# Triangle attention scores: head by head on small tiles of the array, instead of one product with an expanded q

## The reference

```
B, N, _, E = x_in.shape            # 2, 64, 64, 256
H = 8;  d_k = E // H               # 8 heads of 32 channels
q = (x_in @ Wq).reshape(B, N, N, H, d_k)
k = (x_in @ Wk).reshape(B, N, N, H, d_k)
v1 = (x_in @ Wv1).reshape(B, N, N, H, d_k)
v2 = (x_in @ Wv2).reshape(B, N, N, H, d_k)
scores = jnp.einsum('bilhd,bljhd->biljh', q, k) / np.sqrt(d_k)
att = jax.nn.softmax(scores, axis=2)
out = jnp.einsum('biljh,bilhd,bljhd->bijhd', att, v1, v2)
attn_out = out.reshape(B, N, N, E) @ Wo
h = _layer_norm(x_in + attn_out, ln_agg_g, ln_agg_b)
mlp = jax.nn.relu(h @ W1 + b1) @ W2 + b2
return _layer_norm(mlp + h, ln_out_g, ln_out_b)
```

## Time and profile before

| what | value |
|---|---|
| median of three executions | 5114.2 us (5111.48 to 5121.49) |
| the profiled execution | 5109.28 us, its span 5107.6 us |
| PE busy | 4717.0 us, 92% of the span |
| DVE busy | 3492.3 us, 68% |
| ACT busy | 2556.8 us, 50% |
| POOL busy | 2226.1 us, 44% |
| mean granted TensorE clock | 0.965 of full speed |
| score matmuls, line 348 | 1024 records, 385 ns each, 124.6 us of PE busy time |

### The profile page before, as it was taken

How to read it: one execution, slowest core, us unless ns; L and a number is a source line. 1 busy time by engine, 2 the same in 40 slices (tenths; PEclk the granted TensorE clock), 3 DMA queues, 4 the chain that set the end, 5 groups by cost and what they waited for, 6 DMA issues and landing times. The chain is left out here.

```text
span 5107.6 us, 210897 instructions
## 1 busy us (share of the span) xinstructions
PE 4717.0 (92%) x87600; PEld 4048.9 (79%) x87600; DVE 3492.3 (68%) x5697; ACT 2556.8 (50%) x6424; POOL 2226.1 (44%) x1165
## 2 busy tenths in 40 slices
PE   7899989999958999999789999997899989899966
PEld 6788867888845999999569999996788877788866
DVE  3688854888834666666546666663688864788866
ACT  4676646676612333333223333333666746676633
POOL 0599950999933000000320000000499970899930
PEclk9999999999978999999899999998999999999988
DMA  2000011000012000000210000002100012000012
GB/s 80 24 24 24 24 40 52 22 24 24 23 55 69 16 15 15 15 15 12 66 48 16 15 15 15 13 12 70 33 24 24 24 32 60 21 24 24 24 55 86
DMA packets 183401, 162.51 MB, mean 32 GB/s; under 512 B 23472, under 2 KB 178608, under 8 KB 183216
## 3 DMA queue, kind: packets, MB, share of 16 engines
q1 hardware_dynamic: 183216, 159.94, 10.3%
HBM read 109.53 MB, written 50.33 MB: 31 GB/s over the span
## 5 line engine op out<-in xcount | busy, mean ns | idle before, releaser
L812 POOL TENSOR_TENSOR tri_work<-tri_v,tri_work 128x1024 f32<-128x1024 f32 x768 | 1802.5, 2378 | 154.9 <-PE tri_psum L567 154.5
L736 DVE TENSOR_TENSOR tri_work<-tri_v,tri_psum 128x1024 f32<-128x1024 f32 x1280 | 1506.8, 1218 | 215.0 <-PE tri_psum L567 195.0
L567 PE MATMUL tri_psum<-tri_work 128*32 128x64 f32 x65536 | 1104.7, 221 | 39.4 <-issue 17.0
L567 PEld LDWEIGHTS tri_psum<-tri_work 128*32 128x32 f32 x65536 | 964.0, 110 | 197.2 <-issue 105.1
L1238 ACT ACTIVATE global_work<-global_psum 128x512 f32<-128x512 f32 x512 | 306.6, 599 | 1011.7 <-PE global_psum L1199 1011.7
L1313 POOL TENSOR_TENSOR global_work<-global_work,global_bp 128x256 f32<-128x256 f32 x64 | 46.4, 745 | 1576.1 <-DVE global_work L1270 1568.5
L1276 DVE TENSOR_REDUCE global_work<-global_work 128x1 f32<-128x512 f32 x512 | 349.2, 682 | 472.3 <-ACT global_work L1238 472.3
L1219 PE MATMUL global_psum<-global_v_high,global_pT_high 128*128 128x256 f32 x2048 | 610.2, 298 | 4.1 <-DVE global_pT_low L1294 4.1
L1219 PE MATMUL global_psum<-global_v_high,global_pT_low 128*128 128x256 f32 x2048 | 577.1, 282 | 0.0
L1219 PE MATMUL global_psum<-global_v_low,global_pT_high 128*128 128x256 f32 x2048 | 576.7, 282 | 0.0
L1199 PE MATMUL global_psum<-global_k_high,global_q_high 128*128 128x512 f32 x1024 | 421.4, 412 | 24.3 <-DVE global_q_low L1256 21.5
(11 more groups left out here) (140 smaller groups left out, 7815.9 us busy)
## 6 DMA issues: line engine op xcount, KB each, us to landing
tri_work<-in_x SPq DMA_DIRECT2D x192, 128.0 KB, 2.1
tri_work<-x SPq DMA_DIRECT2D x192, 128.0 KB, 2.0
x<-tri_work SPq DMA_DIRECT2D x128, 128.0 KB, 1.7
tri_work<-in_x SPq DMA_DIRECT2D x128, 64.0 KB, 2.2
global_work<-x SPq DMA_DIRECT2D x16, 512.0 KB, 4.2
xn<-global_work SPq DMA_DIRECT2D x16, 512.0 KB, 3.0
qT<-global_work SPq DMA_DIRECT2D x32, 256.0 KB, 2.1
global_work<-qT SPq DMA_DIRECT2D x64, 128.0 KB, 2.2
```

What stands on the lines that cost most here:

```text
L567: mm = nc.tensor.matmul(psum[32 * g:32 * g + 32, OW, region * N:region * N + N], v1_diag[:, c * 32:c * 32 + 32], src[:, at_ * N:at_ * N + ...
L736: nc.vector.tensor_tensor(prod_d[k % 2].rearrange("p (d j) -> p d j", d=CU), v2[:, c:c + CU, :], psum[:, A[n.slot], (c // D) * N:(c // D + ...
L812: nc.gpsimd.tensor_tensor(prod_p[k % 2].rearrange("p (d j) -> p d j", d=CU), v2[:, c:c + CU, :], a_sb[n.slot][:, h * N:(h + 1) * N].unsque ...
```

## The change

q is copied as it is, in one copy on DVE into `qT`, which has the form of kT; the block-diagonal `q_diag`, its zeroing on POOL, the two copies on ACT and the two on DVE are gone, and with them their semaphores. The scores are made head by head: for each l, head r and half t one matmul over the 32 partitions of the head, 64 stationary and 64 moving columns, at the tile position (32 r, 64 t) of the array. That makes 32 matmuls in a group where there were 8. The head r picks the PSUM bank, 4 + r, of which the first 256 columns are used; bank 4 is also the bank of v2. So v2 of a group waits for the score copy of the group before it, and the scores of a group wait for the v2 copies of that group.

```diff
-        q_diag_all = part(2 * 2 * 4 * R * N)
-        q_diag = [q_diag_all[:, k * 8 * R * N:(k + 1) * 8 * R * N].rearrange("p (t l r i) -> p t l r i", t=2, l=4, r=R)
-                  for k in range(2)]
+        qT = [part(2 * 2 * P).rearrange("p (t n) -> p t n", t=2) for _ in range(2)]
...
-                s_psum = psum[:, 6:8, :].rearrange("p a n -> p (a n)")
+                s_psum = psum[:, 4:8, 0:E]
...
-                @block.gpsimd
-                def _(pool):
-
-                    nc.gpsimd.memset(q_diag_all, 0.0).then_inc(s["diag_zero"], 1)
...
-                            pe.wait_ge(s["v2_copy"], after(g - 1))
+                            pe.wait_ge(s["scores_copy"], after(g - 1))
...
-                            pe.wait_ge(s["q0_copy"], after(g))
-                            pe.wait_ge(s["q1_copy"], after(g))
-                            pe.wait_ge(s["scores_copy"], after(g - 1))
+                            pe.wait_ge(s["q_copy"], after(g))
+                            pe.wait_ge(s["v2_copy"], after(g))
                             for l in range(4):
-                                for t in range(2):
-                                    mm = nc.tensor.matmul(s_psum[N * t:N * t + N, l * R * N:(l + 1) * R * N],
-                                                          kT[g.slot][:, t, l * N:l * N + N],
-                                                          q_diag[g.slot][:, t, l].rearrange("p r i -> p (r i)"),
-                                                          start=True, stop=True)
+                                for r in range(R):
+                                    for t in range(2):
+                                        rows = slice(D * r, D * r + D)
+                                        mm = nc.tensor.matmul(s_psum[N * t:N * t + N, r, l * N:l * N + N],
+                                                              kT[g.slot][rows, t, l * N:l * N + N],
+                                                              qT[g.slot][rows, t, l * N:l * N + N],
+                                                              start=True, stop=True, tile_position=(D * r, N * t))
...
-                            if where is None:
-                                act.wait_ge(s["diag_zero"], b + 1 + CREDIT)
-                            for r in range(2):
-                                ins = q_copy(nc.scalar, nxt, r)
-                            ins.then_inc(s["q0_copy"], 1)
...
-                            nc.scalar.activation(scores[:, :, bass.ds((i * 2 + u) * 4, 4)],
-                                                 s_psum.rearrange("p (l n) -> p n l", l=4), ACT.Copy
+                            nc.scalar.activation(scores_i[:, :, :, bass.ds((i * 2 + u) * 4, 4)],
+                                                 s_psum.rearrange("p r (l i) -> p r i l", l=4), ACT.Copy
...
-                            dve.wait_ge(s["kT_copy"], after(nxt))
-                            if where is None:
-                                dve.wait_ge(s["diag_zero"], b + 1 + CREDIT)
-                            dve.wait_ge(s["q0_copy"], after(nxt))
-                            for r in range(2, R):
-                                rows = slice(D * r, D * r + D)
-                                ins = nc.vector.tensor_copy(q_diag[nxt.slot][rows, :, :, r, :],
-                                                            psum[rows, qk_bank[0], :].rearrange("p (t l i) -> p t l i", t=2, l=4))
-                            ins.then_inc(s["q1_copy"], 1)
+                            dve.wait_ge(s["scores_mm"], after(nxt - 2))
+                            nc.vector.tensor_copy(qT[nxt.slot], psum[:, qk_bank[0], :].rearrange("p (t n) -> p t n", t=2)
+                                                  ).then_inc(s["q_copy"], 1)
```

More of the change, by code:

```diff
@@ L234, in _ @@
                 dve.wait_ge(mask_made, 1)
-        names = ("qkv_in", "rows_in0", "rows_in1", "cols_in0", "cols_in1", "diag_zero", "xT_mm", "rowT_copy",
-                 "colT_copy", "v2_mm", "v2_copy", "qk_mm", "kT_copy", "q0_copy", "q1_copy",
+        names = ("qkv_in", "rows_in0", "rows_in1", "cols_in0", "cols_in1", "xT_mm", "rowT_copy",
+                 "colT_copy", "v2_mm", "v2_copy", "qk_mm", "kT_copy", "q_copy",
                  "scores_mm", "scores_copy", "group_max", "maxima",
@@ L329, in body @@
                             pe.wait_ge(s["kT_copy"], after(nxt - 1))
-                            pe.wait_ge(s["q0_copy"], after(nxt - 1))
-                            pe.wait_ge(s["q1_copy"], after(nxt - 1))
+                            pe.wait_ge(s["q_copy"], after(nxt - 1))
                             for bank, wt, src in ((qk_bank[0], wq, colT[nxt.slot]),
@@ L381, in body @@
                                                  ACT.Copy).then_inc(s["kT_copy"], 1)
-                            if where is None:
-                                act.wait_ge(s["diag_zero"], b + 1 + CREDIT)
-                            for r in range(2):
-                                ins = q_copy(nc.scalar, nxt, r)
-                            ins.then_inc(s["q0_copy"], 1)
                         if where is not None:
                             act.wait_ge(s["scores_mm"], after(g))
-                            nc.scalar.activation(scores[:, :, bass.ds((i * 2 + u) * 4, 4)],
-                                                 s_psum.rearrange("p (l n) -> p n l", l=4), ACT.Copy
+                            nc.scalar.activation(scores_i[:, :, :, bass.ds((i * 2 + u) * 4, 4)],
+                                                 s_psum.rearrange("p r (l i) -> p r i l", l=4), ACT.Copy
                                                  ).then_inc(s["scores_copy"], 1)
-                    def q_copy(eng, g, r):
-                        rows = slice(D * r, D * r + D)
-                        return eng.activation(q_diag[g.slot][rows, :, :, r, :],
-                                              psum[rows, qk_bank[0], :].rearrange("p (t l i) -> p t l i", t=2, l=4),
-                                              ACT.Copy)
                     group_steps(act, body)
```

## The result

| kernel | median, us | runs | lowest to highest |
|---|---|---|---|
| before | 5114.94 | 6 | 5111.48 to 5121.49 |
| changed | 5084.48 | 6 | 5076.62 to 5089.14 |

The ratio of changed to before is 0.9939, 95% interval 0.9929 to 0.995: 30 us faster. The forecast was 5060, with a range of 5050 to 5094 that holds the time; the gain is 0.6 of the one that was worked out. The profiled execution of the changed kernel took 5076.62 us with a span of 5075.0, 32.7 us less than the span of before.

A forecast was written before the change was run, and what follows sets the result against it. PE was taken to bound phase 1 of the triangle layers. Four phases of -12.4 us (14 rounds), -1.66 (head) and +0.91 (tail) sum to -52.6 us, giving 5060 us, range 5050 to 5094.

The forecast's parts named there:

- (1): Score burst on PE: eight 32x64 tiles overlap fully, so it takes 0.64 us instead of 1.88; chance 0.70.
- Rival A: Score burst: at most four records at a time, burst 1.09 us, 5087 us; chance 0.13 together with a slowed score copy.
- (2): Shared bank 4: v2 waits for the score copy, still 1.03 us, and starts 1.92 us after the burst's start.
- (3): Scores also wait for v2's copies, which end at 6.42 us, ahead of the scores at 7.20; cover 0.78 us.
- (4): One q copy on DVE (0.69 us) replaces 1.17 on ACT and 1.40 on DVE; it hides in mid-phase.
- (5): Head of a phase: q and k no longer wait for colT behind the q copies; -1.66 us per phase.
- (6): Tail of a phase: the last group's scores wait for its v2 copies to end; +0.91 us per phase.
- Rival B: Score burst: row tiles queue up, burst 1.98 us, round 8.54, 5145 us; chance 0.09.
- the rule: Phase 1 round on PE: its length is the score burst plus 6.56 us.

The follow-up runs named there:

- e6: The kernel of e4 with its score burst cut in two, l = 2 and 3 placed between the q and k matmuls: 5061.0 us in one run.
- e2: The changed kernel with the score burst made twice, 128 records instead of 64, same results written again: 5145.08 us in one run.
- e3: The changed kernel with PE's 16 groups of a phase written out instead of looped: 5078.10 us, ratio to before 0.9931.
- e5: The kernel before with only the shared bank changed (scores in banks 4 and 5, bank 4 shared with v2): 5157.77 us, ratio 1.0082.
- e1: The changed kernel with the score matmuls reordered, heads as the outermost loop: 5121.31 us, ratio to before 1.0017.
- e4: The changed kernel with scores after v2 on PE and ACT, sharing rowT's bank instead of v2's: 5055.49 us, ratio to before 0.9888.

## Why the prediction was right, and where its size was off

The order of the argument held: PE bounds phase 1, the burst shrinks, the score copy comes into the open, and the difference of the two is the gain. Step by step:

(1) The mechanism was right, the size not: full overlap of eight tiles is there (32 records in 0.28 us), but only for the first 32 records. The term "64 / 8 x 0.056 = 0.45, with 0.15 to 0.19 around it: 0.64" measured 0.87. Its first half fits, its second half runs at 31 records in 0.42 us. e6 shows that these records are fast when 1.7 us of large matmuls stand ahead of them, e2 that 64 more records add 0.7 us. Rival A was the nearest to this: it had the pace of a feed, though for all 64 records (1.09), and named no reason why the first 32 should be free of it. A's 5087 is also nearer to the measured 5084 than the 5060 that was said; the range holds the time because it reaches up to A. By the phases alone (-35) the gain lies between A's 24 and the 53 of the sum.

TensorE: Matmul & The Clock Gate in the Trainium skill, in the part "Architectural detail: the array is 16× 32×32, not 1× 128×128", gives TensorE's queue as 64 deep; 32 records with a weight load each, after which the pace breaks, agree with it. That they stand in a queue is argued and not shown. Against its simplest form: at the 11.7 ns a record of e2 an estimated 24 more would have been handed on during the first 0.28 us and be at hand, yet only 6 start in the next 0.14. A queue that is filled again late, or another limit on small records in a row, would fit as well. The floor of about 25 ns between starts, which that page of the Trainium skill has in the part "Wait — 56ns, not 53.3ns?" and which the prediction weighed, doesn't hold for these tiles side by side: 32 records started in 0.28 us, 9 ns each.

(2) Right in kind. The score copy kept its 1.02, the lag to v2 was 0.05, and v2 waits for it. The source view of line 313 has the wait in the rows of the weight loads (PEld) for 32 of the 64 groups, that is in every second round and in the four tails, and in those of the matmuls (PE) 12 times:

```profile
  ACT tri_scores L377: 15.4, 32
...
  ACT tri_scores L377: 5.7, 12
```

(The pauses of 0.38 and 0.33 us, too, that the prediction reads as PE's own stand in the rows of the weight loads; PE's rows show none there.) Two things were missing. v2 started 2.10 after the burst's start instead of 1.92, which is the longer burst; and a matmul that waits for a copy has its first weight load in the open, so v2 to the next scores is 5.38 (63.39 to 68.77) instead of 5.28. That makes 7.48 of 7.20. The prediction had no term at all for the sequencer: with 32 matmuls in the burst the turn of the loop is no longer hidden, which gives the rounds of 7.54 to 7.60, and e3 takes just these away.

```profile
PE tri_psum L306 <- issue: 2.7, 6, 0.5
```

That row, from the waits of PE between 60 and 150 us, is the wait of the transposes: 2.7 us in six rounds, of which only the part beyond the score copy lengthens the round.

(3) Right: the v2 copies were never late in the middle of a phase. (4) Right: the q copy hides; DVE's and ACT's busy shares fell to 38 and 61 of 100 us. (5) Right: -1.74 against -1.66. (6) Nearly: +1.13 against +0.91, again the burst.

The 14 rounds were forecast at -12.4 us a phase and came to -8.2; with head and tail -8.8 instead of -13.2, or -35 instead of -53, of which the two profiled executions show 32.7. The first phase lost 0.70 of it ahead of the transposes of group 1 (40.33 instead of 39.63). That is scatter of the phase's start: from the transposes of group 0 to those of group 1 the four phases differ by +0.7, +0.2, +0.1 and -0.4 us.

Rival B's mechanism is there: e5, with a long burst and the shared bank, has rounds of 8.53 where B has 8.54. That these agree so closely is luck, as e5's burst is 0.1 shorter than B's and the rule 0.1 too short. Its 42 us above before are not B's 33, as e5 keeps the old head and has a longer tail. e1 stands near the point where the change stops paying: a burst of 1.50, with 1.46 worked out, and 5121 against 5113.

What stays open: why the break comes after 32 records, what sets the pace of about 12 ns a record behind it, and why that goes in steps. e2 and e6 show that it is not the records' tiles or banks, but neither looks into the feed itself.

## What to carry to other kernels

A matmul that gets shorter pays only as far as what follows it is not waiting for the copy of its result out of PSUM: place the burst so that long matmuls of another bank come right behind it, as in e4, and pick as the shared bank one whose reader is done by then. Small-tile matmuls side by side need neighbours in different row tiles in program order (e1); here only the first 32 records in a row ran at full pace (e6), and behind 64 of them the turn of PE's loop came into the open (e3). When a wait is put down to "issue", look for what the sequencer has to do there before looking for data.

## What the runs showed of the hardware that was not expected

PE started 32 records of 32x64 tiles, weight loads included, in 0.28 us, and the next ones at about 12 to 14 ns each (31 in 0.42 us; in e2 96 in 1.12 us). Line 567 of before, at 14 ns a record over 128 records, shows no such break (20 records start in each 0.28 us); four tiles side by side use records no faster than that later pace.
